# A state-space scan: gate projections at a chunk's end, output matmuls in its middle, no VectorE copies

## The reference

```python
u, gate = split(h @ W_in.T)                     # 512 -> 2 x 1024
u = silu(causal_conv4(u) + conv_b)
dt, Bm, Cm = split(u @ Wx.T, [32, 16, 16])      # each RMS-normed
delta = softplus(dt @ Wdt.T + dt_bias)          # [L, 1024]
for t in range(L):                              # state [1024, 16]
    state = exp(delta_t * A) * state + (delta_t * u_t) * B_t
    y_t = state @ C_t
y = (y + u * D_param) * silu(gate)
x = x + ga * (y @ W_out.T)
```

## Time and profile before

| | |
|---|---|
| median of 3 runs | 2116.35 us (2115.04 to 2133.87) |
| profiled execution | 2125.84 us, span 2124.0 us |
| busy: TensorE, VectorE, ScalarE, GpSimd | 1695.8, 1449.0, 1089.6, 1042.7 us |
| granted TensorE clock, mean | 0.804 of 2.4 GHz |
| state-space block | from about 815 us to 1983 us; its loop from 912.6 us |

### The profile page before, as it was taken

How to read it: one execution, slowest core, us unless ns; L and a number is a source line. 1 busy time by engine, 2 the same in 40 slices (tenths; PEclk the granted TensorE clock), 3 DMA queues, 4 the chain that set the end, 5 groups by cost and what they waited for, 6 DMA issues and landing times. The chain is left out here.

```text
span 2124.0 us, 24389 instructions
## 1 busy us (share of the span) xinstructions
PE 1695.8 (80%) x8224; PEld 899.6 (42%) x8224; DVE 1449.0 (68%) x2432; ACT 1089.6 (51%) x1988; POOL 1042.7 (49%) x585
## 2 busy tenths in 40 slices
PE   6873999999689975888596887968869687544678
PEld 2510232322265434665273654736547355222332
DVE  3363788887173121079989999899998999988131
ACT  2340666667621112556666566665666756643064
POOL 0000000000053023078998988989889898998102
PEclk8855899999965986887596986969869698556799
DMA  5332000000193446233544435444354443532301
GB/s 207 141 60 39 2 3 3 2 3 3 35 346 113 133 145 227 50 80 80 114 95 96 110 79 107 108 95 110 75 109 110 95 99 83 117 91 62 117 20 60
DMA packets 151262, 192.38 MB, mean 91 GB/s; under 512 B 18245, under 2 KB 123461, under 8 KB 149344
## 3 DMA queue, kind: packets, MB, share of 16 engines
q1 hardware_dynamic: 143250, 168.00, 31.7%
q0 software_dynamic: 4576, 16.79, 2.2%
q10 hardware_dynamic: 3312, 6.03, 0.7%
HBM read 142.60 MB, written 48.18 MB: 90 GB/s over the span
## 5 line engine op out<-in xcount | busy, mean ns | idle before, releaser
L1745 DVE TENSOR_TENSOR_SCAN ssm_scan<-ssm_psum,ssm_state,ssm_scan 128x256 f32<-128x256 f32 x1024 | 683.5, 729 | 26.2 <-ACT ssm_psum L1614 25.9
L1324 POOL TENSOR_TENSOR ssm_scan<-ssm_scan,ssm_bc 128x1024 f32<-128x1024 f32 x256 | 599.8, 2355 | 110.1 <-DVE ssm_state L1748 109.7
L1614 ACT ACTIVATE ssm_psum<-ssm_rep,ssm_a 128x256 f32<-128x256 f32 x1024 | 435.0, 467 | 263.5 <-DVE ssm_scan L1745 262.9
L1448 PE MATMUL ssm_psum<-ssm_scan,ssm_select 128*32 128x256 f32 x2048 | 211.3, 493 | 237.7 <-POOL ssm_scan L1324 232.6
L659 DVE TENSOR_REDUCE att_rowmax<-att_psum 128x1 f32<-128x512 f32 x448 | 278.5, 683 | 73.9 <-PE att_psum L554 73.9
L632 ACT ACTIVATE att_probs<-att_psum 128x1024 f32<-128x1024 f32 x256 | 248.6, 1021 | 151.8 <-PE att_psum L572 151.6
L1309 POOL TENSOR_TENSOR ssm_scan<-ssm_rep,ssm_bc 128x1024 f32<-128x1024 f32 x128 | 301.2, 2354 | 26.8 <-PE ssm_psum L1448 16.6
L1448 PEld LDWEIGHTS ssm_psum<-ssm_scan,ssm_select 128*32 128x32 f32 x2048 | 45.8, 121 | 360.1 <-POOL ssm_scan L1324 263.3
L554 PE MATMUL att_psum<-att_k,att_q 72*128 72x512 bf16 x448 | 161.3, 401 | 35.0 <-DMA att_k<-parts 34.0
L532 POOL COPY att_v<-v_tokens 128x128 f32<-128x128 f32 x8 | 2.3, 292 | 364.6 <-ACT att_out L626 364.6
L1730 DVE TENSOR_TENSOR ssm_scan<-ssm_rep,ssm_psum 128x1024 f32<-128x1024 f32 x128 | 155.5, 1215 | 6.2 <-PE ssm_psum L1448 3.0
(11 more groups left out here) (231 smaller groups left out, 2068.4 us busy)
## 6 DMA issues: line engine op xcount, KB each, us to landing
ssm_rep<-drive_rows SPq DMA_DIRECT2D x256, 256.0 KB, 4.8
qkv_wmod<-in_wmod SPq DMA_DIRECT2D x8, 1536.0 KB, 12.1
moe_we<-in_we SPq DMA_DIRECT2D x8, 1024.0 KB, 14.4
ssm_bc<-bc_rows SPq DMA_DIRECT2D x32, 256.0 KB, 5.2
drive_rows<-ssm_delta SPq DMA_DIRECT2D x64, 128.0 KB, 1.7
drive_rows<-ssm_du SPq DMA_DIRECT2D x64, 128.0 KB, 1.8
sorted_rows<-moe_zeros SPq DMA_DIRECT2D x1, 5888.0 KB, 19.1
moe_sorted<-sorted_rows SPq DMA_DIRECT2D x23, 256.0 KB, 3.4
```

The lines of the kernel that those rows point to most:

```text
L1324: nc.gpsimd.tensor_tensor(scan[:, Q % RING], scan[:, Q % RING], bc[:, c % 2, 1, gr, :].unsqueeze(1).to_broadcast([P, J, SW]), ALU.mult).th ...
L1448: last = nc.tensor.matmul(ps_y[t % 2][32 * j:32 * j + 32, :], select[:], scan[:, Q % RING, j, :], start=(gr == 0), stop=False)
L1614: nc.scalar.activation(ps_decay[n % HALF_BANKS][:, i], rep[:, s % 2, 0, j, :], ACT.Exp, scale=amat[:, t, gr, j:j + 1]).then_inc(decay_done, 1)
L1745: nc.vector.tensor_tensor_scan(scan[:, Q % RING, j, :], ps_decay[(2 * Q + j // 2) % HALF_BANKS][:, j % 2], scan[:, Q % RING, j, :], state[ ...
```

## The change

- `y` is written into the gate's buffer in place of one of its own; `h` gets a second buffer; `du` holds all eight tiles, and GpSimd makes it two tiles at a time, in slots 26, 27, 29 and 30 for the next chunk.
- Gate projections move from slots 10, 11, 12, 14 to 28 to 31; ScalarE copies them in slots 30, 31 and in 0, 1 of the next chunk, and their Silu moves from slot 20 to slot 4 of the chunk that uses them. Output matmuls move from 16, 17, 27, 29 to 11, 14, 17, 20, residuals to 13, 16, 19, 22. Steps move one slot later.
- The gates of chunk 0 leave the head for slots 0 to 3 of chunk 0's loop, ahead of that slot's other extra step; the norm of chunk 1 goes among the head's other steps.
- `rms_wide` goes. In its place ScalarE's inverse root runs three times with a broadcast input and writes the wide tile.

```diff
-        AT = {..., 10: ("gate", 0), 11: ("gate", 1), 12: ("gate", 2), 13: ("rows", 0), 14: ("gate", 3), 15: ("square", 0),
-              16: ("out", 0), 17: ("out", 1), 18: ("var", 0), 19: ("rms", 0), 20: ("bcast", 0), 21: ("step", 0), 22: ("step", 1),
-              24: ("step", 2), 25: ("step", 3), 27: ("out", 2), 29: ("out", 3)}
+        AT = {..., 11: ("out", 0), 13: ("rows", 0), 14: ("out", 1), 15: ("square", 0), 17: ("out", 2), 18: ("var", 0), 19: ("rms", 0),
+              20: ("out", 3), 21: ("bcast", 0), 22: ("step", 0), 23: ("step", 1), 25: ("step", 2), 26: ("step", 3),
+              28: ("gate", 0), 29: ("gate", 1), 30: ("gate", 2), 31: ("gate", 3)}
-        FIRST = (..., ("conv", 0, 3), ("gate", 0, 0), ("gate", 0, 1), ("rows", 0, 0), ("gate", 0, 2), ("square", 0, 0),
-                 ("gate", 0, 3), ("rms", 0, 0), ("step", 0, 0), ("step", 0, 1), ("step", 0, 2), ("step", 0, 3),
-                 ("mean", 1, 0), ("var", 1, 0), ("bcast", 1, 0))
+        FIRST = (..., ("conv", 0, 3), ("mean", 1, 0), ("rows", 0, 0), ("square", 0, 0), ("var", 1, 0), ("rms", 0, 0),
+                 ("step", 0, 0), ("step", 0, 1), ("step", 0, 2), ("step", 0, 3), ("bcast", 1, 0))
+        FIRST_GATES = range(MP)
 ...
+            steps = [("gate", 0, q)] if c == 0 and q in FIRST_GATES else []
 ...
-        GATE_OUT = {13: 0, 14: 1, 15: 2, 17: 3}
-        SILU, ROWS_OUT, RMS, SQUARE, GATE_SILU, RSTD, H_OUT = 13, 16, 18, 19, 20, 21, 24
-        STEP_OUT = {24: 0, 25: 1, 27: 2, 28: 3}
+        GATE_OUT = {30: 0, 31: 1}
+        SILU, ROWS_OUT, RMS, SQUARE, GATE_SILU, RSTD, H_OUT = 13, 16, 18, 19, 4, 21, 26
+        GATE_LATE = {0: 2, 1: 3}
+        STEP_OUT = {25: 0, 26: 1, 28: 2, 29: 3}
-        CENTRED, RMS_WIDE, NORMED, NORM = 10, 18, 21, 22
-        DELTA = {24: 0, 25: 1, 27: 2, 28: 3}
-        RESIDUAL = {18: 0, 19: 1, 29: 2, 31: 3}
-        GATE_Y, DRIVE = 2, 1
+        CENTRED, NORMED, NORM = 10, 21, 23
+        DELTA = {25: 0, 26: 1, 28: 2, 29: 3}
+        RESIDUAL = {13: 0, 16: 1, 19: 2, 22: 3}
+        DRIVE = {26: 0, 27: 1, 29: 2, 30: 3}
 ... inverse_rms, ScalarE
-                nc.scalar.activation(flat, flat, ACT.Exp, scale=-0.5).then_inc(rms_done, 1)
+                for s, (at, n) in enumerate(((0, RANK), (RANK, NST), (RANK + NST, NST))):
+                    nc.scalar.activation(rwide[:, :, at:at + n], rms[:, :, s:s + 1].to_broadcast([P, ST, n]), ACT.Exp, scale=-0.5).then_inc(rwide_done, 1)
 ... drive_input, GpSimd
-                nc.gpsimd.tensor_tensor(du[:, s % 2], delta[:, t, :], u[:, c % 2, t, :], ALU.mult).then_inc(du_done, 1)
+                nc.gpsimd.tensor_tensor(du[:, sl], delta[:, sl], u[:, c % 2, sl], ALU.mult).then_inc(du_done, 1)
 ... gate_y, VectorE
-                nc.vector.tensor_tensor(y[:, c % 2, t, :], ps_y[t % 2], gate[:, c % 2, t, :], ALU.mult).then_inc(ygate_done, 1)
+                nc.vector.tensor_tensor(gate[:, c % 2, t, :], ps_y[t % 2], gate[:, c % 2, t, :], ALU.mult).then_inc(ygate_done, 1)
 ... ScalarE, in slot q of chunk c
+                    if c >= 1 and q in GATE_LATE:
+                        copy_gate(c, GATE_LATE[q])
+                    if c == 0 and q - 1 in FIRST_GATES:
+                        copy_gate(0, q - 1)
+                    if q == GATE_SILU:
+                        silu_gate(c)
 ... ScalarE, head
             silu_u(0)
-            copy_gate(0, 0)
-            copy_gate(0, 1)
+            squares(1)
             copy_rows(0)
-            copy_gate(0, 2)
+            inverse_sd(1)
             inverse_rms(0)
-            copy_gate(0, 3)
             for pair in range(DP):
                 step_out(0, pair)
-            silu_gate(0)
-            norm_chunk(1)
+            modulate(1)
```

More of the change, by code:

```diff
@@ L1176, in at @@
                 if 0 <= c + AHEAD[kind] < SCH:
-                    return kind, c + AHEAD[kind], i
-            return None
-        ORDER = list(FIRST) + [at(c, q) for c in range(SCH) for q in range(UNITS) if at(c, q)] + [("out", SCH - 1, i) for i in range(MP)]
+                    steps.append((kind, c + AHEAD[kind], i))
+            return steps
+        ORDER = list(FIRST) + [step for c in range(SCH) for q in range(UNITS) for step in at(c, q)] + [("out", SCH - 1, i) for i in range(MP)]
         PLACE = {key: n for n, key in enumerate(ORDER)}
@@ L1310, in spread @@
                                         bc[:, c % 2, 0, gr, :].unsqueeze(1).to_broadcast([P, J, SW]), ALU.mult).then_inc(pool_input, 1)
-            drive_input(0, 0)
-            drive_input(0, 1)
+            for pair in range(DP):
+                drive_input(0, pair)
             for Q in range(2):
@@ L1325, in _ @@
                                             bc[:, c % 2, 1, gr, :].unsqueeze(1).to_broadcast([P, J, SW]), ALU.mult).then_inc(read_done, 1)
[L1326 to L1328 removed]
+                    if c + 1 < SCH and q in DRIVE:
+                        drive_input(c + 1, DRIVE[q])
         @block.tensor
@@ L1335, in released @@
                     return centred_done, c + 1
+                if kind == "step":
+                    return delta_done, c * DP + i + 1
                 if kind == "var":
@@ L1388, in project @@
                     for k in range(KT):
-                        last = nc.tensor.matmul(halves("proj", c, pair)[:, i], win[:, k, m:m + P], h[:, k, :], start=(k == 0), stop=(k == KT - 1))
+                        last = nc.tensor.matmul(halves("proj", c, pair)[:, i], win[:, k, m:m + P], h[:, c % 2, k, :], start=(k == 0), stop=(k == KT - 1))
                 last.then_inc(proj_done, 1)
@@ L1430, in gate_project @@
                     for k in range(KT):
-                        last = nc.tensor.matmul(halves("gate", c, pair)[:, i], win[:, k, m:m + P], h[:, k, :], start=(k == 0), stop=(k == KT - 1))
+                        last = nc.tensor.matmul(halves("gate", c, pair)[:, i], win[:, k, m:m + P], h[:, c % 2, k, :], start=(k == 0), stop=(k == KT - 1))
                 last.then_inc(gate_mm, 1)
@@ L1437, in output @@
                 for t in range(DT):
-                    last = nc.tensor.matmul(bank("out", c, m)[:, 0:SW], wout[:, t, m * P:(m + 1) * P], y[:, c % 2, t, :], start=(t == 0), stop=(t == DT - 1))
+                    last = nc.tensor.matmul(bank("out", c, m)[:, 0:SW], wout[:, t, m * P:(m + 1) * P], gate[:, c % 2, t, :], start=(t == 0), stop=(t == DT - 1))
                 last.then_inc(out_mm, 1)
@@ L1484, in _ @@
                     pe.wait_ge(diag_done, DT * (TAPS + 1))
-                if (kind, i) == ("gate", 0):
-                    pe.wait_ge(win_in, 48)
                 misc(kind, c, i)
+            pe.wait_ge(win_in, 48)
             for c in range(SCH):
                 for q in range(UNITS):
-                    if at(c, q):
-                        misc(*at(c, q))
+                    for step in at(c, q):
+                        misc(*step)
                     sum_states(c, q)
```

74 lines of the change are left out of this document (31 added, 43 removed).

## The result

The changed kernel takes 2153.46 us (median of 4 runs, 2148.12 to 2154.57) against 2115.69 (2110.3 to 2133.87) in the same comparison: ratio 1.0153, 95% interval 1.0102 to 1.0204. That is slower, and outside the range of the prediction.

What follows compares the result with a forecast made beforehand. The prediction took VectorE to lead, GpSimd close behind, neither full, with VectorE's waits for TensorE and ScalarE mattering as much as its work. Its terms summed to +1 on the median of 2116.35, so 2117 us, no change; range 2085 to 2148.

Steps and rivals of the forecast that it cites:

- head: Ahead of the loop: with chunk 0's gates out, the first scan starts earlier, near 901; -13 us.
- gates in chunk 0: Slots 0 to 4 of chunk 0: scans lose time to gate work, +19 us; fewer waits before slot 10, less 3.
- copies: VectorE's copies into `rwide` go, and ScalarE's extra exponentials cost nothing; -28 us.
- gates at a chunk's end: Slots 30 to 1: gates fetched only two slots later make VectorE wait 5.0 us at each of seven boundaries; +35 us.
- gate's Silu in slot 4: Slot 4: Silu delays decays 2.2 us a chunk, partly offset in slots 13 and 20; net 0.6, seven times, +4.
- middle: Slots 3 to 9 and the centring: TensorE on time, so their waits go or shrink in six chunks; -20 us.
- output matmuls and residuals: Slots 11 to 22, residuals two slots after outputs: waits of 4.2 us a chunk where 2.65 stood; +10 us.
- steps: Steps one slot later: ScalarE's modulation comes ahead of the second pair, so a wait of 1.24 becomes 0.8; -3 us.
- rival of *2153: Chunk boundaries: gate pairs 1 to 3 take 5.43 us at the half clock, not 3.72; +36 us, chance 0.18.
- All the copies' time comes back: Rival: copies' 28 us come off whole and each boundary costs 1 us, not 5; 2089 us, chance 0.28.
- third rival: `rwide` copies were waiting for GpSimd and what follows waits instead; 25 of 28 us not gained, 2142 us, chance 0.08.

Runs made afterwards that it cites:

- e5: Changed kernel with extra matmuls, their result overwritten, in TensorE's lulls of chunks 1 to 6: 2129.19 us, ratio 1.0053.
- e2: Changed kernel with each VectorE residual update one slot later (14, 17, 20, 23): 2091.91 us, ratio 0.9862.
- e9: Changed kernel with the centring in slot 11 and not 10: 2126.19 us, ratio 1.0040.
- e1: Kernel before with only the wide inverse RMS copies moved from VectorE to ScalarE exponentials: 2099.60 us, ratio 0.9894.
- e8: Changed kernel with residuals one slot later and half of the gate matmuls left out, so the gate differs from the reference's: 2096.58 us, ratio 0.9895.
- e3: Changed kernel with ScalarE's gate copies one slot later, three slots after the projections: 2143.96 us, ratio 1.0105.

## Why the prediction was wrong

By its own terms, summed over the block from the two traces (waits after less waits before; microseconds):

| term | predicted | measured |
|---|---|---|
| head | -13 | -12.2 |
| gates in chunk 0 | +19, less 3 | +20.6, less 3.0 |
| copies | -28 | -27.3 |
| gates at a chunk's end | +35 | +35.0 |
| gate's Silu in slot 4 | +4 | -1.1 |
| middle | -20 | -10.7 |
| output matmuls and residuals | +10 | +24.8 |
| steps | -3 | -1.7 |
| sum | +1 | +24.4 (block: +23.2) |

Waits under 0.3 us stand in no term; they fell by 1.0, most of what lies between the sum and the block. By the prediction's own way of counting the block alone gives 2116 + 23 = 2140 us, inside its range of 2085 to 2148. That the median is 2153, outside, is owed, as far as one profiled execution of each shows, to the 14.6 us beyond the block, whose cause is open. The forecast of no change was wrong either way: the block is 23 us longer.

**The step that failed is the output matmuls,** "two slots later, +10". I took 4.2 us a chunk, between 0.8 and 5.9; it is 7.0, above my upper bound, and 51.1 in all against 26.3. The bound let two outputs run at the half clock and gave the fourth half the extra. In the trace the fourth also comes after a lull (2.19 us idle) and runs whole at 5.53, behind sums and a skip that are at the half clock too (1.08 and 1.22; 0.64 and 0.70 at the full clock). In the earlier trace rows the 5.96 is an output's, though I read it as a pair of projections, and I did not ask what the residual could do about it. e5 shows that the clock makes the outputs late, e2 that this costs only because the residual stands where it must wait: a slot later, the two outputs that are still slow cost nothing. The Trainium skill (TensorE: Matmul & The Clock Gate, Loop structure matters more than you think) says that the loop nest decides whether matmuls stay at the fast clock, and that a long wait for a DMA ahead of each loses it; the trace agrees, with waits for GpSimd: 0.67 granted from 1400 to 1440 us, where the longer ones take 2.2 to 4.4 us. I had that rule as a rival, but put its price at the gates.

**The second miss is the middle.** TensorE was on time when slot 3 began: the first convolution, at 1340.05, had waited 2.08 us for GpSimd. The scans' waits of slots 3 to 9 did go (10.7). But from there TensorE runs five pairs and the mean without a pause to 1365.7, longer than VectorE needs for these slots, so the centring in slot 10 waits 2.71 as before. An earlier start was not to be had, as the stretch now begins with a wait for GpSimd; e9, a later centring, helped. And 1.7 us of this stretch are the clock again: behind the lull the first convolution takes 5.4 in each of six chunks, and 3.72 in the kernel before. The first two rows are of the changed kernel, the last of the one before:

```profile
1339.48 0.64 PE L1449 MATMUL ssm_psum<-ssm_scan,ssm_select 128*32 128x256 f32 x8 [2.08 <-POOL ssm_scan L1326]
1340.05 5.41 PE L1398 MATMUL ssm_psum<-ssm_upre,ssm_conv 128*128 128x256 f32 x16
```

```profile
1326.12 3.72 PE L1397 MATMUL ssm_psum<-ssm_upre,ssm_conv 128*128 128x256 f32 x16
```

No run tried the stretch of the changed kernel at the full clock throughout, so whether the centring would then wait 1.0, as forecast, is open.

The Silu is the small one the other way, but not a gain: the 1.5 of slot 13 was hidden behind the residual of that slot, and 1.0 of it is back in e2. The rival of *2153* named the right time for a wrong reason: its gate pairs take 4.86, 3.72, 3.72 and 3.72. *All the copies' time comes back* was right on the copies (e1) and wrong on the gates, whose boundary costs what I said. In that there is some luck: of the 4.4 that I added up, the parts 0.6, 2.0, 1.2 and 0.6 (slots 30, 31, 0, 1) came as 2.28, 1.35, 1.02 and 0.47, and the first gate pair was slow:

```profile
1446.97 4.86 PE L1432 MATMUL ssm_psum<-ssm_h,ssm_win 128*128 128x256 f32 x16
```

With a first pair of 5.43 the 0.6 would have become 2.3 by that sum, and not the 3.0 that I put. That the boundary is TensorE's affair, which I argued for e8, e3 and e8 did not bear out: what sets it is open.

## What to carry to other kernels

Where engines work strictly in order, give the reader of a matmul a place that the slow case of that matmul still meets: here one slot, a one-line change, was worth 47 us, more than any other part. If steps are spread thin, allow for TensorE's slow clock at every one of them that follows a lull (here 2.1 to 3.4 us long), and count it whole in the upper bound. And a change made of many parts is worth taking apart: the copies' move alone with later residuals gives 2065 us, while the rest, and by its waits the move of the gates above all, costs some 21 in the block.

## What the hardware showed that I had not expected

A copy of 32 or 64 elements takes 1.24 us on average before, and the trace counts that as busy. Ahead of the loop, where GpSimd does nothing, three of them take 0.37. In the loop all 21 end 0.04 to 0.06 us after the end of a GpSimd instruction. The three of the earlier trace rows, taken singly in the trace, end at 1381.50, 1383.80 and 1384.49; GpSimd's read-outs and product in the second fence end at 1381.45, 1383.76 and 1384.45.

```profile
881.37 0.37 DVE L1708 COPY ssm_rwide<-ssm_rms 128x64 f32<-128x64 f32 x3 [21.36 <-ACT ssm_rms L1563]
```

```profile
1379.08 4.68 POOL L1324 TENSOR_TENSOR ssm_scan<-ssm_scan,ssm_bc 128x1024 f32<-128x1024 f32 x2
1383.70 0.74 POOL L1298 TENSOR_TENSOR ssm_du<-ssm_delta,ssm_u 128x256 f32<-128x256 f32 x1
```

The Trainium skill (SBUF — State Buffer, Who interferes with whom) says that a VectorE copy between SBUF tiles can need a port pair that it shares with GpSimd, held for a whole instruction while the other is blocked, and that ScalarE never waits for it. The trace agrees: the same values written by ScalarE take 0.21 us each (0.26 for the 64 elements), in the loop too, minimum, median and maximum in ns:

```profile
L1566 ACT ACTIVATE ssm_rwide<-ssm_rms x24: 212/213/256, 885.6 to 1801.1; 128x32 f32<-128x32 f32 x16, 128x64 f32<-128x64 f32 x8
```

So the copies did wait for GpSimd, as the third rival has it, and yet what follows them does not wait in their place.
